# A decoder layer with a gated delta rule: a decay multiply and a scaling on POOL, and a product over 96 columns

## What is computed

```python
def step(st, inp):
    qt, kt, vt, gt, bt = inp
    st = st * jnp.exp(gt)[..., None, None]
    pred = jnp.einsum('bhd,bhdv->bhv', kt, st)
    delta = (vt - pred) * bt[..., None]
    st = st + jnp.einsum('bhd,bhv->bhdv', kt, delta)
    ot = jnp.einsum('bhd,bhdv->bhv', qt, st)
    return (st, ot)
...
o = o * jax.nn.silu(z)
o = o * jax.lax.rsqrt(jnp.mean(o * o, -1, keepdims=True) + EPS) * norm_w
return o.reshape(b, s, HV * DV) @ w_o
```

## Time and profile before

| | |
|---|---|
| median of 3 runs | 2828.41 us (2825.41, 2828.41, 2831.17) |
| span of the profiled execution | 2822.2 us |
| busy, share of the span | PE 78%, PEld 65%, DVE 72%, ACT 45%, POOL 31% |
| mean granted clock of TensorE | 0.898 |
| attention passes | from 156 to about 1930 us of the span |
| DMA | mean 24 GB/s |

### The profile page before, as it was taken

One profiled execution on the slowest core, in us unless ns is written; L12 is line 12 of the kernel. 1 busy time (PEld: TensorE's weight loads), 2 busy tenths in 40 slices (PEclk: granted clock), 3 DMA queues, 4 the chain that ended last, 5 costly groups with the idle time before them and its releaser, 6 DMA issues. The chain is left out here.

```text
span 2822.2 us, 50077 instructions
## 1 busy us (share of the span) xinstructions
PE 2198.1 (78%) x16224; PEld 1831.0 (65%) x16254; DVE 2034.6 (72%) x3600; ACT 1281.7 (45%) x3113; POOL 878.9 (31%) x1339
## 2 busy tenths in 40 slices
PE   4667888788779888887788888862388788887888
PEld 2466777677668767776677677762166665665666
DVE  5778888978878889788788897752464655646555
ACT  3345546456455464564554545431334333343333
POOL 2526346255263362552643625512000000000000
PEclk8889999999999999999899999986589899889899
DMA  2000000000000000000000000002312212122120
GB/s 58 5 5 16 11 4 11 4 15 11 4 15 11 4 11 4 15 11 4 15 11 4 11 4 12 1 1 57 93 44 57 51 47 66 43 56 52 46 64 5
DMA packets 71633, 67.70 MB, mean 24 GB/s; under 512 B 26814, under 2 KB 61342, under 8 KB 71582
## 3 DMA queue, kind: packets, MB, share of 16 engines
q1 hardware_dynamic: 71582, 67.06, 9.3%
HBM read 51.81 MB, written 14.68 MB: 24 GB/s over the span
## 5 line engine op out<-in xcount | busy, mean ns | idle before, releaser
L1002 POOL TENSOR_TENSOR blk_inv<-blk_inv,blk_tmp 128x31 f32<-128x31 f32 (+15 forms) x496 | 316.4, 638 | 38.9
L823 DVE SCALAR_TENSOR_TENSOR v_t<-cbank,cwv,v_t 128x504 f32<-128x504 f32 (+2 forms) x384 | 279.6, 732 | 39.2 <-ACT v_t L680 30.0
L823 DVE SCALAR_TENSOR_TENSOR kq<-cbank,cwq,kq 128x504 f32<-128x504 f32 (+2 forms) x384 | 279.1, 730 | 39.3 <-ACT kq L680 30.2
L981 POOL TENSOR_TENSOR knorm_next<-k,power 128x4 f32<-128x4 f32 x64 | 64.5, 1008 | 704.0 <-DVE k L839 704.0
L1000 POOL TENSOR_TENSOR blk_tmp<-blk,blk_inv 128x31 f32<-128x31 f32 (+15 forms) x496 | 264.4, 533 | 36.6
L554 PE MATMUL bbank<-bm,t_bd 128*128 128x128 f32 x1024 | 156.4, 316 | 149.3 <-DVE t_bd L873 135.9
L554 PEld LDWEIGHTS bbank<-bm,t_bd 128*128 128x128 f32 x1024 | 146.2, 226 | 156.5 <-DVE t_bd L873 114.9
L718 ACT ACTIVATE vals<-og 128x128 f32<-128x128 f32 x512 | 151.0, 296 | 204.2 <-DVE og L891 201.6
L1349 PE MATMUL sbank<-kpad,qst 128*128 128x512 f32 x256 | 121.9, 547 | 78.7 <-DVE mx L1575 48.0
L1693 POOL TENSOR_SCALAR rs<-mv 128x1 f32<-128x1 f32 x16 | 3.4, 213 | 567.3 <-DVE mv L1595 567.3
L873 DVE STREAM_TRANSPOSE t_bd<-blk_inv 32x1024 f32<-32x1024 f32 x64 | 139.1, 2174 | 43.6 <-POOL blk_inv L1002 42.9
(11 more groups left out here) (236 smaller groups left out, 6761.8 us busy)
## 6 DMA issues: line engine op xcount, KB each, us to landing
wv_raw<-in_L_attn_w_qkvz_dram SPq DMA_DIRECT2D x16, 512.0 KB, 3.4
kst<-k_stacks SPq DMA_DIRECT2D x64, 96.0 KB
qst<-q_stacks SPq DMA_DIRECT2D x64, 96.0 KB
kpad<-k_stacks SPq DMA_DIRECT2D x64, 96.0 KB
qpad<-q_stacks SPq DMA_DIRECT2D x64, 96.0 KB
wq_raw<-in_L_attn_w_qkvz_dram SPq DMA_DIRECT2D x16, 256.0 KB, 2.5
wo_s<-in_L_attn_w_o_dram SPq DMA_DIRECT2D x16, 256.0 KB, 2.6
k_stacks<-kq_hi SPq DMA_DIRECT2D x128, 32.0 KB
```

Source lines behind the costliest of these rows:

```text
L823: ins = dve.scalar_tensor_tensor(view[:, :, back:], proj[:, :, 0:S - back], taps[:, TAPS - 1 - back:TAPS - back], view[:, :, back:], ALU.m ...
L1002: ins = pool.tensor_tensor(inv[:, j + 1:, 0:upto], inv[:, j + 1:, 0:upto], tmp[:, 0:below, 0:upto], ALU.subtract)
```

## The change

Three edits, none in the lists of pieces.

1. The product for `bm` is one DVE instruction a chunk instead of 8. For that, POOL multiplies the chunk's part of `decay` by `coef` in place beforehand, a new share of POOL in QK c, with a semaphore `dk`. DVE waits for it before `bm`, and before it writes `coef` anew.
2. The scaling SC c of `og` by `rstd_o` is issued by POOL instead of DVE.
3. B1 forms columns 32 to 127 only.

```diff
-    "QK": dict(kk_ps=1, bm=1),
+    "QK": dict(kk_ps=1, dk=1, bm=1),
...
-                        mm = pe.matmul(bbank[:, bank, j, :], t_bd[:, c * PPC + j, :], bm[:, c * PPC + j, :],
+                        mm = pe.matmul(bbank[:, bank, j, HB:], t_bd[:, c * PPC + j, :], bm[:, c * PPC + j, HB:],
                                        start=True, stop=True)
...
+                    if not start or c:
+                        dve.wait_ge(sem["dk"], w.at("dk"))
                     dve.tensor_tensor(coef[:], beta.rearrange("p (t g) -> p t g", g=G),
...
-                    dve.wait_ge(sem["coef"], w.at("coef"))
-                    dve.wait_ge(sem["e_ex"], e_ex_of(w, start))
-                    for t in range(TPC):
-                        for g in range(G):
-                            n = c * PPC + t * G + g
-                            ins = dve.scalar_tensor_tensor(
-                                bm[:, n, :].rearrange("p (a t) -> p a t", a=2), kk[:, t, :].rearrange("p (a t) -> p a t", a=2),
-                                coef[:, t, g:g + 1], decay[:, n:n + 1, :].to_broadcast([P, 2, S]), ALU.mult, ALU.mult)
-                    ins.then_inc(sem["bm"], 1)
+                    dve.wait_ge(sem["dk"], w.at("dk", 1))
+                    own = slice(c * PPC, (c + 1) * PPC)
+                    dve.tensor_tensor(bm[:, own, :].rearrange("p (t g) (a s) -> p t g a s", g=G, a=2),
+                                      kk.rearrange("p t (a s) -> p t a s", a=2).unsqueeze(2).to_broadcast([P, TPC, G, 2, S]),
+                                      decay[:, own, :].rearrange("p (t g) s -> p t g s", g=G).unsqueeze(3
+                                                                 ).to_broadcast([P, TPC, G, 2, S]),
+                                      ALU.mult).then_inc(sem["bm"], 1)
...
-                elif kind == "SC":
-                    dve.wait_ge(sem["rstd"], w.done("rstd", "RS", arg))
-                    dve.tensor_tensor(og[:], og[:], rstd_o[:].unsqueeze(2).to_broadcast([P, PPC, DK]),
-                                      ALU.mult).then_inc(sem["osc"], 1)
...
+                elif kind == "QK":
+                    c = arg
+                    own = slice(c * PPC, (c + 1) * PPC)
+                    pool.wait_ge(sem["coef"], w.at("coef"))
+                    pool.wait_ge(sem["e_ex"], e_ex_of(w, start))
+                    pool.tensor_tensor(decay[:, own, :], decay[:, own, :],
+                                       coef[:].rearrange("p t g -> p (t g)").unsqueeze(2).to_broadcast([P, PPC, S]),
+                                       ALU.mult).then_inc(sem["dk"], 1)
+                elif kind == "SC":
+                    pool.wait_ge(sem["rstd"], w.done("rstd", "RS", arg))
+                    pool.tensor_tensor(og[:], og[:], rstd_o[:].unsqueeze(2).to_broadcast([P, PPC, DK]),
+                                       ALU.mult).then_inc(sem["osc"], 1)
```

## The result

The changed kernel takes 3084.15 us, the median of 4 runs (3080.93 to 3085.78), against 2829.79 us for the kernel before (4 runs, 2825.41 to 2832.80). The ratio of the runs is 1.0909, with a 95% interval of 1.0890 to 1.0928 (the two medians alone give 1.0899). The span of the profiled execution is 3082.0 us at a mean granted clock of 0.857 (before 2822.2 and 0.898). The forecast was 3081 us with a range of 3025 to 3135, so the time came out 3 us above it.

What follows compares the result with a forecast made beforehand. DVE was taken to pace the early half of each period, POOL's chain after TIN the late half. Terms summed to +16.8 us a period, times fifteen 252, plus 1, on 2828.4: 3081 us, range 3025 to 3135.

Steps and rivals of the forecast that it cites:

- The round trip: Late half, scaling 2 through PE, DVE and ACT to RS 3's power: POOL idles 14.3 us a period, no longer hidden.
- The half clock: PE at TO 2 after some 14 us idle: runs slow as after TOUT's idle, 2.25 us more in the round trip.
- The scalings: Scalings of chunks 2 and 3 in POOL's queue between INV2 and INV3: 2.1 us each, 2.2 with the hop.
- Contention: Inverse steps on POOL beside DVE's scalings of chunks 2 and 3: gone twice a period, −1.7 us.
- The start of the chain: Early half up to QK 3's end: gains nothing, +0.2 us a period (from −3 to +2), QN 3 2.0 earlier.
- DVE saves 3 × 0.94: Early half, QK 0 to 2 on DVE: one instruction instead of eight saves 0.94 us a chunk, not all arriving.
- The idle before RS 2: POOL before the power of RS 2: 0.5 us idle mostly closes as chunk 2's gate comes earlier, −0.4 us.
- B1: Early half, PE's product over 96 columns: saves between nothing and 0.5 us (0.9 for chunk 0), counted as zero.
- Only POOL's own work counts: Rival 1, late half: the round trip stays hidden, 2.5 us a period, 2867 us in all; chance 6%.
- DVE's relief decides: Rival 2, at QK 3: multiply and round trip hide, TIN starts 2.9 us earlier, −0.6 a period, 2819 us; chance 3%.
- The round trip is costlier: Rival 3: half clock covers all 7.64 us to the gate, both scalings meet contention, period +23.9, 3188 us; chance 5%.
- The multiply is no gain: Rival 4: QK 3 ends up to 1 us later, chunks 0 to 2 give nothing, 3119 us; chance 4%.

Runs made afterwards that it cites:

- the first experiment: The changed kernel with the scaling of og back on DVE, against the kernel before: 2874.06 us against 2823.18, ratio 1.0174.
- the wait-only kernel: The kernel before, with DVE's scaling of chunk 2 also waiting for the end of INV2, against the kernel before: 3038.23 us against 2823.18, ratio 1.0753.
- the mixed version: Kernel before with POOL's multiply for chunks 0 to 2, scalings 0 and 1 on POOL, B1 over 96 columns, against the kernel before: 2823.40 us against 2824.00.
- the fastest one: The kernel before with scalings 0 and 1 on POOL, 2 and 3 on DVE, against the kernel before: 2802.25 us against 2824.62, ratio 0.9922.

## Why the prediction was right

**Bound and places.** Of the +16.9 us of a period, 16.2 lie where the prediction put them, on POOL's chain from the memset on, and in it the wait at the power of RS 3; 0.7 lie ahead of it. Moving one instruction took it away, and the wait alone brought it without the work.

**The round trip** was put at 14.3 us and measured 13.84. Its parts: the first hop 1029.41 − (1027.37 + 1.90) = 0.14 instead of 0.37, transposes to gate 9.70 instead of 7.64 + 2.25 = 9.89, gate to POOL 3.99 instead of 4.0. The half clock was the boldest part of it, carried over from TOUT's idle to one that did not exist yet. The window from the transposes on shows it.

```profile
1029.41:1033.71 4.30, 4.30 (x14) 0.50 0.00 0
1033.71:1035.51 1.80, 1.80 (x17) 0.94 0.00 0
```

**The scalings** took 1.90 us instead of 2.1, nearest to the low bound from E's product (1.83), not to the slopes of the inverse (2.02, 2.35). With their hops both came to 3.9 instead of 4.4. The Trainium skill's figure (GPSIMD Engine Reference, Elementwise — side-by-side cycle accounting), by which one was estimated at 2.25 us, is higher still; the measurement decides.

**Contention** was put at −1.7. INV1 with INV2 became 1.0 shorter and INV3 0.8, together −1.8, and the long step of INV3 is gone (1136 to 729 ns at 247 elements). One long step stays, 1.36 us at 902.78 before and 1.32 us at 1004.50 here, where about 0.5 is usual: it lies beside DVE's split of a weight in a high and a low part, not beside a scaling. The scaling of chunk 3 still runs beside DVE's work and takes 1.90 as well.

**The start of the chain** is where the terms were off, by little. QK 3 ended 59.6 us after TOUT, +0.8 instead of +0.2: QN 3 came 1.3 us earlier, not 2.0. The step that failed is "DVE saves 3 × 0.94": none of it arrived at QN 3 in the first experiment, where DVE waits for PE and ACT instead. The idle before RS 2 was to close by 0.4 and grew from 0.51 to 0.80, because OO 2 ran at half clock (3.68 us above, 1.98 for the like one) after PE had idled 3.52. These two lie 0.6 and 0.7 above their terms; the smaller scalings and round trip take back 1.0, TIN and the contention 0.2: 16.8 predicted, 16.9 measured.

**Luck.** That the time came out within 3 us is luck in part, since errors of 1.3 and −1.2 us a period cancel. Over all fifteen periods the loss is 257.0 us instead of 252. Outside them the stretch before the first TOUT became 2.4 us shorter and that after the last 5.3 longer (0 and 1 in the forecast; not followed up), and the span of the profiled executions grew by 259.8, the medians by 254.

**B1** was put at zero, between nothing "if loading weights sets the pace" and 0.5. The lower end is right for the product. That a narrower product could go with a slower kernel was not in my bounds; with 96 columns it is 4.6 us in all, and none of it in the periods once they have settled.

**The rivals.** *Only POOL's own work counts* (2867 us) falls by the wait-only kernel, which is as slow without any of that work. With scaling 2 moved early, however, the same theory nearly holds: 2877 us. *DVE's relief decides* (2819) falls as a whole, but its condition was nearly met by the version with scalings 0 and 1 on POOL, which inserts nothing between INV0 and INV3 and is faster, as that rival had it. *The round trip is costlier* (3188) falls by 9.70 us to the gate. Its counterargument was read short, though: after TOUT PE worked at half clock for 4.6 us (to 13.4 us after TOUT), not 3.8, and for about 4.5 in the round trip. *The multiply is no gain* (3119) was half right in its mechanism, not in its size: QK 3 ends 0.8 us later and chunks 0 to 2 give nothing, but the rest does not follow. Without the scaling's move, the multiply and B1 cost 51 us; in the change the relief from scaling 0 covers most of what QK 3 loses, and so +0.2 looked harmless.

## What to carry to other kernels

When an instruction moves to an engine that takes its queue in order, read off its neighbours in that queue first, and price the wait of everything that needs its result; the scalings' own durations came to 3.8 us a period here and the place of one of them to 13.6. Ask which engine's next instruction in that queue depends on the moved one through the others: that closes the loop. Of a move of four equal pieces, keep those that fall where the new engine is idle and the old one paces (two of four gave −0.8%, all four +7.5%), and count no relief on an engine whose next instruction already waits for somebody.

## What the runs showed of the hardware

- A POOL product in place with one operand read from 8 elements a partition takes 1897 ns for 1024 elements and 1045 for 512, 1.66 ns an element over 193 fixed; the subtraction of the inverse with two full operands costs 2.09 ns an element.
- On POOL a power of 8 elements a partition takes 1.64 us and one of 4 takes 1.01, as much as a product over 512 or more. They are what the multiply stood behind.
- The fp32 product with 128 × 128 weights takes nearly the same time over 64, 96 and 128 columns: 1.89, 1.92 and 1.95 us for 16 passes at full clock.
- The time at which PE's clock comes back to full after TOUT differs in kernels that differ little and in periods of one kernel: 13.4 us after TOUT before, 15.3 in the mixed version, 11.7 and 13.9 in turn in the fastest one, and in threes with 64 columns. It moves a period by up to 1 us, and a total by some 20. So a difference of less than 1% between two such kernels can be the clock's timing and not the work of the edit. What sets it stayed open.
